# Relative-position attention on one core: heads regrouped by every fourth, the first batch's near terms stored in four parts, and two schedules moved

## The chip, the core and the metric

The kernel runs on one NeuronCore of a Trainium2 chip. That core has TensorE (PE) for matmuls, VectorE (DVE), ScalarE (ACT) and GpSimd (POOL) for elementwise work, SyncE (SP), which issues most of the transfers, and 16 DMA engines between on-chip memory (SBUF, 128 partitions) and HBM. The metric is the device time of one launch in microseconds (us); less is better.

## The reference, cut to what matters

The network is a chain of six sublayers on a token array of 4 batches x 512 tokens x 128 channels. The change touches only the second sublayer, the disentangled attention of layer 0, with 16 heads of 8 channels:

```python
q, k, v = split_heads(x @ Wq + bq), split_heads(x @ Wk + bk), split_heads(x @ Wv + bv)
scores  = einsum('bhqd,bhkd->bhqk', q, k) / scale
pos_k   = (rel_embeddings @ Wk + bk)                       # 64 rows per head
c2p = take_along_axis(einsum('bhqd,hpd->bhqp', q, pos_k), clip(rel + 32, 0, 63), -1)
p2c = take_along_axis(einsum('bhkd,hpd->bhkp', k, pos_k), clip(-rel + 32, 0, 63), -1).swapaxes(-1, -2)
probs = softmax(scores + (c2p + p2c) / scale, -1)          # 4 x 16 x 512 x 512
out = layernorm((probs @ v merged) @ Wo + bo + x)
```

`rel` depends only on the distance of query and key. Within 64 tokens of the diagonal it takes many values ("near"); farther out it is one constant on each side ("far").

## The kernel before

**Tables.** For each batch, 12 matmuls ("chunks", `row_products`) make the position products of q and k, 5 of 112 rows and 1 of 128 rows for each side. ScalarE copies each into one of four `rows` buffers (`copy_rows`) and SP stores it to HBM (`store_chunk`). SP loads them back turned by block (`load_rows`: `load_q_rows`, `load_k_rows`, ten loads or places a batch), so that partition 8h+n holds head h and block n of 64 queries.

**Near terms.** `near_build` adds pairs of these rows into the tile `near`: 128 partitions of 64 x 192 floats, 48 KB each. VectorE builds batch 0, GpSimd batches 1 to 3. The tile goes to HBM (`dram["near"]`): batch 0 by one DMA of 128 rows of 48 KB from SP (`store_first_near`), the others by GpSimd in four pieces of 16 of the 64 queries each (`LATER_PIECES`), and GpSimd waits for every piece before it goes on.

**Attention.** The work is 16 groups n = 4b + g of four heads of one batch; each group is four quads (q = 4n + t, a tile of 128 queries, four heads). For a quad PE makes four score matmuls (`score`), VectorE adds the near terms from `bias` and takes the row maximum (`add_terms`, L1442), ScalarE takes the exponential, PE transposes, PE multiplies with v, VectorE divides (`close_heads`, L1453). SP feeds this: `load_tiles(n)` brings the stacked q and k of a group (128 rows of 2 KB, two buffers), and `load_bias(n, t)` brings the near terms of quad t of group n as two DMAs, each into 64 partitions, 4 heads x 192 floats per partition. `bias` has one buffer for each t, so a load waits until quad t of the group before has been added (`neg_ready`); it thus runs a group ahead.

**Order of the work.** Each engine has one list in order. SP: chunks and row loads of batch 0, `load_tiles(0)`, the near store, a wait for all of it (the store is issued by L1203, the wait is L1249), the eight bias loads of group 0, four more chunks, then the loop over groups and quads, into which `late_quad` puts the 24 chunks of batches 2 and 3 (one after each of the quads 1 to 24) and `ROW_STEPS` the row loads of batches 1 to 3. GpSimd: it waits until batch 0's near store has landed (its build overwrites `near`) and until the first four row loads of batch 1 are there, builds batch 1, stores it, and so on. SP's wait at L1270 stands before the first bias load of batches 1, 2 and 3 and asks for all pieces of that batch.

All of SP's DMAs go into one queue (q1 in the rows below); GpSimd's have a queue of their own (q0). Most move 112 or 128 rows. Two early ones, the zeros that `store_edges` writes into the margins of the tables, have an outermost extent of 6 on both sides (6 x 4 rows of 384 floats, 36 KB each).

## Time and profile before

| | us |
|---|---|
| median of 3 runs (lowest, highest) | 788.75 (788.44, 790.29) |
| the profiled execution | 788.52 |
| its span from first to last instruction | 786.8 |
| busy: PE, DVE, ACT, POOL | 583.0, 531.2, 437.1, 219.6 |
| feed-forward and tables before the attention's quads | 0 to 162 |
| wait for the first near terms | 162 to 180 |
| 64 quads of attention | 180 to 476 |
| the four sublayers after it | 476 to 787 |

The profile page gives one execution. Busy time of an engine says little by itself; the timeline and the waits say which instruction released which. Times in the rows are us from the start of the span.

### The profile page before, as it was taken

The page shows a single profiled execution, that of the slowest core. Times are in us where ns is not written, and L with a number is a line of the kernel's source. Part 1 is how long each engine was busy: PE and PEld are TensorE (multiplying, and loading weights), DVE is VectorE, ACT ScalarE, POOL GpSimd, SP SyncE. Part 2 cuts the span into 40 slices and gives each one's busy share as a digit, 9 for nine tenths or more (in the row PEclk, how much of TensorE's full clock was granted, in tenths as well). Part 3 has the DMA queues.
Part 4 walks back from the last instruction along what each step waited for, and adds up shares of the span by engine and source line. Part 5 has one row for each costly group of instructions (what it writes and reads, how often), then busy time and mean ns, then how long its engine had stood idle before and what let it go on. Part 6 is the DMA issues. An engine that isn't in the chain of part 4 may idle for free. (4 is left out here: it accounts for less than half of the span.)

```text
span 786.8 us, 16609 instructions
## 1 busy us (share of the span) xinstructions
PE 583.0 (74%) x5220; PEld 417.2 (53%) x5220; DVE 531.2 (68%) x1878; ACT 437.1 (56%) x944; POOL 219.6 (28%) x274
## 2 busy tenths in 40 slices
PE   4499927727999999999999998343993661686660
PEld 3387923324666566667666666233982451364460
DVE  7612235815787678989999995771226888766887
ACT  2034524415888788888888884631551523464522
POOL 1743422000950391095040000056442100212000
PEclk9999977866999999999999998655997655799655
DMA  8669525989989899999954413725552000000001
GB/s 251 179 182 391 185 79 169 289 342 269 283 274 335 220 278 348 324 225 271 338 157 129 124 48 99 165 76 146 180 166 71 0 1 1 0 1 2 0 1 53
DMA packets 133602, 130.79 MB, mean 166 GB/s; under 512 B 29565, under 2 KB 109485, under 8 KB 131853
## 3 DMA queue, kind: packets, MB, share of 16 engines
q1 hardware_dynamic: 126668, 103.61, 46.3%
q0 software_dynamic: 4736, 25.07, 8.7%
q10 hardware_dynamic: 2112, 1.05, 0.5%
q8 instruction: 44, 0.72, 0.4%
q14 instruction: 42, 0.34, 0.1%
HBM read 73.43 MB, written 52.92 MB: 161 GB/s over the span
## 5 line engine op out<-in xcount | busy, mean ns | idle before, releaser
L1442 DVE CUSTOM_DVE_ANT_0 l0am_prob<-l0am_ps_s,l0am_bias 128x512 f32<-128x512 f32 x256 | 161.6, 687 | 56.1 <-PE l0am_ps_s L1519 34.9
L1361 ACT ACTIVATE l0am_prob<-l0am_prob,l0am_neg_top 128x512 f32<-128x512 f32 x256 | 172.1, 730 | 19.1 <-DVE l0am_neg_top L1442 19.0
L1531 PE MATMUL l0am_ps_t<-c_ident,l0am_prob 128*128 128x128 f32 x1024 | 138.2, 279 | 0.0
L1531 PEld LDWEIGHTS l0am_ps_t<-c_ident,l0am_prob 128*128 128x128 f32 x1024 | 113.8, 142 | 16.7 <-issue 16.6
L1355 ACT COPY l0am_probT<-l0am_ps_t 128x512 f32<-128x512 f32 x128 | 69.0, 590 | 45.6 <-PE l0am_ps_t L1531 45.6
L1519 PE MATMUL l0am_ps_s<-l0am_ks,l0am_qs 32*128 32x512 f32 x512 | 74.0, 647 | 21.7 <-DVE l0am_neg_top L1442 19.5
L1429 DVE COPY l0am_probT<-l0am_ps_t 128x512 f32<-128x512 f32 x128 | 82.2, 683 | 2.5 <-PE l0am_ps_t L1531 2.4
L764 DVE COPY l0f_xsT<-l0f_psT 128x128 f32<-128x128 f32 x46 | 13.4, 292 | 97.5 <-PE l0f_psT L872 97.5
L593 ACT ACTIVATE l0f_h<-l0f_psU,l0f_experts 128x128 f32<-128x128 f32 x184 | 52.6, 368 | 47.2 <-PE l0f_psU L882 47.2
L1544 PE MATMUL l0am_ps_c<-l0am_probT,l0am_v 128*9 128x128 f32 x2048 | 67.9, 273 | 0.9 <-issue 0.9
L509 POOL DMA_INDIRECT token_results<-l0f_ys,l0f_token_i x46 | 44.3, 962 | 62.5 <-DVE l0f_ys L774 61.9
L882 PE MATMUL l0f_psU<-l0f_xsT,l0f_mine 128*128 128x128 f32 x368 | 55.3, 297 | 4.2 <-issue 1.8
L1142 POOL TENSOR_TENSOR l0am_near<-l0am_rows_q,l0am_rows_k 128x352 f32<-128x352 f32 (+7 forms) x24 | 31.3, 1336 | 96.2 <-DMA l0am_rows_k<-position_k 86.8
L1544 PEld LDWEIGHTS l0am_ps_c<-l0am_probT,l0am_v 128*9 128x9 f32 x2048 | 49.5, 90 | 11.7 <-issue 11.6
L1151 POOL TENSOR_TENSOR l0am_near<-l0am_rows_q,l0am_rows_k 128x192 f32<-128x192 f32 (+6 forms) x96 | 54.0, 608 | 0.2
L882 PEld LDWEIGHTS l0f_psU<-l0f_xsT,l0f_mine 128*128 128x128 f32 x368 | 48.6, 206 | 8.3 <-issue 4.9
L499 POOL DMA_INDIRECT sorted_tokens<-l0f_xn,l0f_pos_i x32 | 31.4, 980 | 56.7 <-DVE l0f_pos_i L665 47.9
L1519 PEld LDWEIGHTS l0am_ps_s<-l0am_ks,l0am_qs 32*128 32x128 f32 x512 | 20.2, 184 | 47.8 <-issue 25.4
L1552 PEld LDWEIGHTS l0am_ps_g<-c_ident,l0am_headT 128*128 128x128 f32 x64 | 9.0, 140 | 48.2 <-issue 28.8
L1481 PE MATMUL l0am_ps_s<-l0am_xnT,l0w_wext 128*112 128x512 f32 (+1 forms) x48 | 27.2, 726 | 4.5 <-ACT l0am_rows L1337 3.8
L893 PE MATMUL l0f_psR<-l0f_experts,l0f_h 128*128 x192 | 27.1, 286 | 1.7 <-ACT l0f_h L593 1.7
L1337 ACT ACTIVATE l0am_rows<-l0am_ps_s,l0w_row_bias 112x512 f32<-112x512 f32 (+1 forms) x24 | 16.1, 687 | 20.6 <-PE l0am_ps_s L1481 7.2
(312 smaller groups left out, 976.6 us busy)
## 6 DMA issues: line engine op xcount, KB each, us to landing
l0am_bias<-near_terms SPq DMA_DIRECT2D x128, 192.0 KB, 4.8
near_terms<-l0am_near POOLq DMA_DIRECT2D x12, 1536.0 KB, 8.3
l0f_mine<-l0f_experts SPq DMA_DIRECT2D x46, 256.0 KB, 2.8
l0am_rows_k<-position_k SPq DMA_DIRECT2D x16, 448.0 KB, 6.9
near_terms<-l0am_near SPq DMA_DIRECT2D x1, 6144.0 KB, 19.8
position_q<-l0am_rows SPq DMA_DIRECT2D x20, 224.0 KB, 4.8
position_k<-l0am_rows SPq DMA_DIRECT2D x20, 224.0 KB, 4.9
l0am_rows_q<-position_q SPq DMA_DIRECT2D x20, 224.0 KB, 6.0
```

What stands on the lines that cost most here:

```text
L499: pool.indirect_dma_start(xs_dram[:, :], bass.IndirectOffsetOnAxis(ap=pos_i[:, t:t + 1], axis=0), xn[:, t, 0:XS_COLS], None).then_inc(scat ...
L509: pool.indirect_dma_start(ys_dram[:, :], bass.IndirectOffsetOnAxis(ap=token_i[:, s:s + 1], axis=0), ys[:, s % UNROLL, :], None).then_inc(y ...
L593: last = nc.scalar.activation(h[:, j, k, :], psU[:, s % 2, k, :], ACT.Gelu_apprx_tanh, bias=part_of(row, SLAB_B1 + k, 1))
L882: last = pe.matmul(psU[:, s % 2, k, :], mine[:, j, k * P:(k + 1) * P], xsT[:, j, :], start=True, stop=True)
L1151: last = engine.tensor_tensor(view(near, at, (WIN + 1, 64), (1, width)), view(rows_q, ROW_OF[pq] * 64, (1, 64), (0, width)), view(rows_k, ...
L1355: nc.scalar.copy(probT[:, u // GROUP % 2, u % GROUP, :, :], ps_t[:, u % 2, :, :]).then_inc(copied_act, 1)
L1361: nc.scalar.activation(prob[:, k, :], prob[:, k, :], ACT.Exp, bias=neg_top[:, k:k + 1], scale=-1.0)\
L1429: dve.tensor_copy(probT[:, u // GROUP % 2, u % GROUP, :, :], ps_t[:, u % 2, :, :]).then_inc(copied_dve, 1)
L1442: dve.tensor_tensor_reduce(out=prob[:, k, :], in0=ps_s[:, j, :], in1=bias[:, j, at:at + S], scale=-1.0, scalar=HUGE, op0=ALU.add, op1=ALU.min,
L1519: pe.matmul(ps_s[:, j, :], qs[r, n % 2, t * P:t * P + P], ks[r, n % 2, :], start=True, stop=True, tile_position=(32 * j, 0)).then_inc(scor ...
L1531: last = pe.transpose(ps_t[:, u % 2, i, :], prob[:, u % SLOTS_, i * P:(i + 1) * P], ident[:, :])
L1544: last = pe.matmul(ps_c[32 * j:32 * j + DH + 1, 0:P], v[:, T4 * b + i, GROUP * g + j, :], probT[:, q % 2, j, i, :], start=(i == 0), stop=( ...
```

## The change

Four things change. (1) A group now holds the heads g, g+4, g+8, g+12 instead of 4g to 4g+3; so `load_tiles`, `load_bias`, the v columns and the place of the result take other strides, and the source of `load_tiles` is now four blocks of 32 rows. (2) Batch 0's near terms go out group by group: `store_first_near(g)` issues four DMAs, one a head, of 8 partitions (rows of 48 KB) each. Group 0's bias loads wait only for its own four; the stores of groups 1, 2 and 3 are issued later in SP's list, and GpSimd waits for all 16 DMAs before it builds batch 1. The first two of batch 1's row loads move ahead of that wait, and the next two to right behind group 0's bias loads. (3) GpSimd's four pieces become two. (4) Batch 3's chunks go to quads 15 to 26 instead of 13 to 24 (quads 13 and 14 get none), and its row loads to 24 to 33 instead of 21 to 30.

```diff
-LATER_PIECES = tuple((q0, q0 + 16) for q0 in range(0, 64, 16))
+LATER_PIECES = ((0, 32), (32, 64))
-    for later, quads in ((1, [-1, -1, 0, 0, 1, 1, 2, 2, 3, 3]), (2, range(9, 19)), (3, range(21, 31))):
+    for later, first, quads in ((1, 2, [-4, -4, 0, 1, 1, 2, 2, 3]), (2, 0, range(9, 19)), (3, 0, range(24, 34))):
         for place, quad in enumerate(quads):
-            steps.setdefault(divmod(quad + T4, T4), []).append((later, place))
+            steps.setdefault(divmod(quad + T4, T4), []).append((later, first + place))
...
+        LAST = 3 * BATCH_CHUNKS
-        first_near_out = sem("first_near_out")
+        first_near_out = [sem(f"first_near_out{g}") for g in range(GROUPS)]
+        FIRST_STORES = GROUP
         def late_quad(cn):
-            return cn - EARLY + 1
+            return cn - EARLY + 1 if cn < LAST else cn - LAST + 15
...
-                def store_first_near():
+                def store_first_near(g):
                     part = 64 * WIN
-                    own = [(part, P), (1, part)]
-                    sp.dma_start(bass.AP(dram["near"].tensor, 0, own), bass.AP(near[:, :].tensor, 0, own)).then_inc(first_near_out, 16)
+                    own = [(part, NB), (1, part)]
+                    for j in range(GROUP):
+                        at = (GROUPS * j + g) * NB * part
+                        sp.dma_start(bass.AP(dram["near"].tensor, at, own), bass.AP(near[:, :].tensor, at, own)).then_inc(first_near_out[g], 16)
...
                     for side, dst in enumerate((qs, ks)):
-                        src = bass.AP(dram["stack"][side].tensor, MARGIN + n * GROUP * 32 * FAR_PITCH, [(FAR_PITCH, P), (1, S)])
+                        b, g = divmod(n, GROUPS)
+                        src = bass.AP(dram["stack"][side].tensor, MARGIN + (b * HEADS + g) * 32 * FAR_PITCH,
+                                      [(GROUPS * 32 * FAR_PITCH, GROUP), (FAR_PITCH, 32), (1, S)])
...
-                        src = bass.AP(dram["near"].tensor, n * GROUP * (NB * 64 * WIN) + (2 * t + s) * (64 * WIN),
-                                      [(WIN, 64), (NB * 64 * WIN, GROUP), (1, WIN)])
+                        src = bass.AP(dram["near"].tensor, (b * HEADS + g) * (NB * 64 * WIN) + (2 * t + s) * (64 * WIN),
+                                      [(WIN, 64), (GROUPS * NB * 64 * WIN, GROUP), (1, WIN)])
...
                 sp.wait_ge(near_dve, 1)
-                store_first_near()
+                store_first_near(0)
+                load_rows(1, 0)
+                load_rows(1, 1)
                 sp.wait_ge(filled, 1)
-                sp.wait_ge(first_near_out, 16)
+                sp.wait_ge(first_near_out[0], 16 * FIRST_STORES)
                 for t in range(T4):
                     load_bias(0, t)
+                store_first_near(1)
...
                             sp.wait_ge(neg_ready, 16 * (n - 1) + 4 * (t + 1))
-                            if g == 0 and t == 0:
+                            if b == 0 and t == 0:
+                                sp.wait_ge(first_near_out[g], 16 * FIRST_STORES)
+                            elif g == 0 and t == 0:
                                 sp.wait_ge(near_out, 16 * len(LATER_PIECES) * b)
                             load_bias(n, t)
-                        for cn in range(EARLY, B * BATCH_CHUNKS):
-                            if n and late_quad(cn) == 4 * (n - 1) + t:
-                                store_chunk(cn)
+                        if (n, t) in ((0, 1), (1, 0)):
+                            store_first_near(2 + n)
+                        if n and T4 * (n - 1) + t in late:
+                            store_chunk(late[T4 * (n - 1) + t])
...
                     if b == 1:
-                        pool.wait_ge(first_near_out, 16)
+                        for g in range(GROUPS):
+                            pool.wait_ge(first_near_out[g], 16 * FIRST_STORES)
...
-                    dve.tensor_tensor(heads_out[:, t, n, :].rearrange("p (j d) -> p j d", j=GROUP), by_head[:, :, 0:DH],
+                    b, g = divmod(n, GROUPS)
+                    own = heads_out[:, t, GROUPS * b:GROUPS * b + GROUPS, DH * g:DH * g + DH]
+                    dve.tensor_tensor(own, by_head[:, :, 0:DH],
...
-                            last = pe.matmul(ps_c[32 * j:32 * j + DH + 1, 0:P], v[:, T4 * b + i, GROUP * g + j, :],
+                            last = pe.matmul(ps_c[32 * j:32 * j + DH + 1, 0:P], v[:, T4 * b + i, GROUPS * j + g, :],
```

PE and ScalarE take the chunk of quad q from the dictionary `late` instead of computing `EARLY + q - 1`.

## Rows read from the trace of the kernel before

**Rows 1.** Windows of three stages: busy us per engine, TensorE clock, DMA share, GB/s.
```profile
156.00:180.00 24.00, 6.89 (x45) 4.72 (x43) 2.77 (x4) 3.41 (x5) 0.00 (x0) 0.69 0.83 325
180.00:264.00 84.00, 81.26 (x888) 50.05 (x892) 63.12 (x185) 67.42 (x125) 30.67 (x44) 0.95 0.97 279
...
346.00:476.00 130.00, 129.90 (x1760) 89.84 (x1759) 123.97 (x373) 113.68 (x217) 29.36 (x39) 1.00 0.61 175
```
**Rows 2.** Timeline of all engines around the start of the attention (start us, us).
```profile
153.82 0.34 SPq L1220 DMA_DIRECT2D l0am_qs<-stacked_q  x1
...
155.69 0.43 SPq L1203 DMA_DIRECT2D near_terms<-l0am_near  x1
...
162.58 1.14 PE L1519 MATMUL l0am_ps_s<-l0am_ks,l0am_qs 32*128 32x512 f32 x8 [0.83 <-issue]
...
175.59 5.28 SPq L1227 DMA_DIRECT2D l0am_bias<-near_terms  x8
180.16 0.69 DVE L1442 CUSTOM_DVE_ANT_0 l0am_prob<-l0am_ps_s,l0am_bias 128x512 f32<-128x512 f32 x1 [17.67 <-DMA l0am_bias<-near_terms]
```
**Rows 3.** Windows while one kind of transfer runs: near-term store, then bias loads.
```profile
158.00:172.00 14.00, 4.89 (x41) 3.82 (x39) 2.77 (x4) 2.55 (x3) 0.00 (x0) 0.75 1.04 446
178.00:184.00 6.00, 1.26 (x8) 0.51 (x8) 2.53 (x8) 2.56 (x4) 0.00 (x0) 0.50 1.10 224
```
**Rows 4.** DMA issues of the whole span: out<-in, count, KB each, us to landing.
```profile
l0am_bias<-near_terms SPq DMA_DIRECT2D x128, 192.0 KB, 4.8
near_terms<-l0am_near POOLq DMA_DIRECT2D x12, 1536.0 KB, 8.3
...
l0am_rows_k<-position_k SPq DMA_DIRECT2D x16, 448.0 KB, 6.9
near_terms<-l0am_near SPq DMA_DIRECT2D x1, 6144.0 KB, 19.8
...
l0am_qs<-stacked_q SPq DMA_DIRECT2D x16, 256.0 KB, 4.4
...
position_q<-in_block_rows SPq DMA_DIRECT2D x1, 36.0 KB
position_k<-in_block_rows SPq DMA_DIRECT2D x1, 36.0 KB
```
**Rows 5.** DMA queues from 97.5 to 98.9 us: packets, MB, share of 16 engines.
```profile
q1 hardware_dynamic: 60, 0.07, 15.2%
```
**Rows 6.** Timeline, VectorE: first reduction of quads 4, 5 and 16.
```profile
200.88 0.69 DVE L1442 CUSTOM_DVE_ANT_0 l0am_prob<-l0am_ps_s,l0am_bias 128x512 f32<-128x512 f32 x1 [1.06 <-PE l0am_ps_s L1519]
...
206.00 0.69 DVE L1442 CUSTOM_DVE_ANT_0 l0am_prob<-l0am_ps_s,l0am_bias 128x512 f32<-128x512 f32 x1 [1.05 <-PE l0am_ps_s L1519]
...
263.68 0.69 DVE L1442 CUSTOM_DVE_ANT_0 l0am_prob<-l0am_ps_s,l0am_bias 128x512 f32<-128x512 f32 x1 [2.35 <-issue]
```
**Rows 7.** Timeline of GpSimd: build and stores of batch 1's near terms.
```profile
197.90 10.45 POOL L1142 TENSOR_TENSOR l0am_near<-l0am_rows_q,l0am_rows_k 128x352 f32<-128x352 f32 x8 [71.75 <-DMA l0am_rows_k<-position_k]
...
226.71 0.61 POOL L1290 DMA_DIRECT2D near_terms<-l0am_near  x1 [0.31 <-POOL l0am_near L1151]
...
251.97 0.53 POOL L1290 DMA_DIRECT2D near_terms<-l0am_near  x1 [7.95 <-DMA near_terms<-l0am_near]
```
**Rows 8.** Timeline of SyncE: the first bias load of batch 1.
```profile
259.40 1.25 SPq L1227 DMA_DIRECT2D l0am_bias<-near_terms  x2
```
**Rows 9.** Waits of SyncE's own queue: us in total, times, longest us.
```profile
SPq L1249 <- DMA near_terms<-l0am_near: 19.4, 1, 19.4
...
SPq L1270 <- DMA near_terms<-l0am_near: 10.6, 3, 8.3
```
**Rows 10.** Timeline, VectorE: closing step of quads 25, 30, then 46 and 47.
```profile
325.46 0.19 DVE L1453 TENSOR_TENSOR l0a_heads<-l0am_ps_g,l0am_rate 128x32 f32<-128x32 f32 x1
...
348.79 0.19 DVE L1453 TENSOR_TENSOR l0a_heads<-l0am_ps_g,l0am_rate 128x32 f32<-128x32 f32 x1
...
416.10 0.19 DVE L1453 TENSOR_TENSOR l0a_heads<-l0am_ps_g,l0am_rate 128x32 f32<-128x32 f32 x1
...
420.32 0.19 DVE L1453 TENSOR_TENSOR l0a_heads<-l0am_ps_g,l0am_rate 128x32 f32<-128x32 f32 x1
```

More of the change, by code:

```diff
@@ L1125, in late_quad @@
         def late_quad(cn):
-            return cn - EARLY + 1
+            return cn - EARLY + 1 if cn < LAST else cn - LAST + 15
+        late = {late_quad(cn): cn for cn in range(EARLY, B * BATCH_CHUNKS)}
         def view(what, offset, *dims):
@@ L1382, in _ @@
                         exp(4 * q + 3)
-                    cn = EARLY + q - 1
-                    if EARLY <= cn < B * BATCH_CHUNKS:
-                        copy_rows(cn, ps_g[:, :])
+                    if q in late:
+                        copy_rows(late[q], ps_g[:, :])
             @block.vector
@@ L1452, in close_heads @@
                     dve.wait_ge(rates_ready, q + 1)
-                    dve.tensor_tensor(heads_out[:, t, n, :].rearrange("p (j d) -> p j d", j=GROUP), by_head[:, :, 0:DH],
+                    b, g = divmod(n, GROUPS)
+                    own = heads_out[:, t, GROUPS * b:GROUPS * b + GROUPS, DH * g:DH * g + DH]
+                    dve.tensor_tensor(own, by_head[:, :, 0:DH],
                                       rate[:, :].unsqueeze(2).broadcast_to((P, GROUP, DH)), ALU.mult).then_inc(heads_ready, 1)
@@ L1556, in _ @@
                         score(q)
-                    cn = EARLY + q - 2
                     if 3 <= q:
-                        if EARLY <= cn < B * BATCH_CHUNKS:
-                            pe.wait_ge(rows_ready, cn + 1)
+                        if q - 1 in late:
+                            pe.wait_ge(rows_ready, late[q - 1] + 1)
                         turn_heads(q - 3)
@@ L1569, in _ @@
                         turn(4 * (q - 1) + 3)
-                    cn = EARLY + q - 1
-                    if EARLY <= cn < B * BATCH_CHUNKS:
-                        if cn == EARLY + 1:
-                            pe.wait_ge(rows_ready, cn)
+                    if q in late:
+                        if late[q] == EARLY + 1:
+                            pe.wait_ge(rows_ready, late[q])
                         if 3 <= q:
                             pe.wait_ge(heads_ready, q - 2)
-                        row_products(cn, ps_g[:, :])
+                        row_products(late[q], ps_g[:, :])
         clear_semaphores(nc, own_sems + aside.own_sems)
```

## The prediction

> **What bounds the kernel now.** I read the windows first. The attention is 64 quads from 180 to 476 us, with PE at 97 to 100% in each window [rows 1], in lockstep with VectorE and ScalarE. A quad takes 4.22 us without table work (416.10 to 420.32 [rows 10]) and 5.12 us with a chunk in it (200.88 to 206.00 [rows 6]). The change removes no chunk, so this pace stays.
>
> What it can move are the waits around it. The timeline shows the first: PE has the first scores at 162.58, but VectorE's first reduction starts at 180.16, after 17.67 us of waiting for a bias load; the load was issued at 175.59, 19.9 us after the near store was issued at 155.69 [rows 2], and SP's queue was waiting for that store for 19.4 us of it [rows 9]. A second is small: SP waits 8.3 us for the near terms of batch 1 [rows 9], issues their load at 259.40 [rows 8], and quad 16 starts at 263.68 [rows 6]. At the usual pace from quad 5 it would be 206.00 + 11 x 5.12 = 262.4, so 1.3 us are lost. A third: quads 26 to 30 took 348.79 - 325.46 = 23.3 us for 5 x 4.22 = 21.1 [rows 10], so 2.2 us are lost.
>
> Behind quad 16 stands a chain: GpSimd starts batch 1's build at 197.90, stores it from 226.71 on (28.8 us of build), and the four stores are through at 259.4, 32.7 us later [rows 7, 8]. From there to quad 16 are 4.3 us. That chain had 4 us to spare at most. GpSimd may start only when all of batch 0 is stored, which is long done before. After the change it isn't.
>
> **The price that decides: a group's store.** It is 4 DMAs of 8 partitions x 48 KB, 1.57 MB. I call its time g. The whole store (6144 KB, 6.29 MB [rows 4]) ran at 446 GB/s [rows 3], 14.1 us for its bytes; the other 5.8 us of its 19.9 were what was queued ahead of it, and its landing. Nothing in the trace stores so few partitions, so I bound it.
>
> - Best: it goes over all 16 engines like the whole one: 1.57 MB at 446 GB/s, g = 3.5 us.
> - Engines: two early DMAs of 24 rows with outermost extent 6 (36 KB each [rows 4]) left 60 packets on q1 [rows 5], 48 rows and 12 more, 6 a DMA. A counting packet from each engine used gives 6 engines, not 16 (with 16 it would be 80 packets). So an outermost extent of 8 gives 8 engines: g = 7.1 us.
> - Worst: the rate also goes by the partitions. While only bias loads run, each into 64 partitions, all engines are as busy as with the store (DMA share 1.10 against 1.04), but move 224 GB/s instead of 446 [rows 3]: half the partitions, half the rate. In proportion, 8 partitions get 27.9 GB/s, so one DMA takes 14.1 us: g = 14.1 if the four run at once, 56.4 if one after another.
>
> The bias row is the nearest one, so I stay with its rule. Between its two readings I take the geometric middle, g = 28.2 us: the four follow one another on the same engines, but a part of the 8 partitions may have a path of its own.
>
> The Trainium skill speaks against this change here. SBUF — State Buffer, section "Door 1: The DMA port swizzle", says that a transfer's rate goes by how many of 16 ports its partitions reach, about 27 GB/s a port, that partitions 0 to 63 reach 8 of them, and by its table an aligned block of 8 reaches 2. The trace agrees for 64 partitions (224 GB/s); for 8 no row here shows it. By it one DMA would take about 7.2 us and, as an estimate, the four in a row 29 us.
>
> **The change part by part.**
>
> *Tile loads.* Their source's outermost extent becomes 4, so by the same reading they use 4 engines: 2 x 256 KB at a quarter of 446 GB/s are 4.7 us instead of 1.2, +3.5. `load_tiles(0)` lies right ahead of the near store in the queue [rows 2], so that much is added there.
>
> *Start.* Group 0 stored: 155.7 + 5.8 + 3.5 + g = 165.0 + g. Then 4.6 us for its bias load (175.59 to 180.16 [rows 2]): with g = 28.2 the first quad is at 197.8, 17.6 us later than now.
>
> *Up to GpSimd's start.* Behind that moment SP's queue holds, in order: group 0's bias, 1.57 MB at 224 GB/s, 7.2 us; store 1, g; four chunks, 0.95 MB at 279 GB/s [rows 1], 3.5; two row loads, 0.67 MB, 2.3; store 2, g; tiles of group 1, 4.7; the first bias of group 1, 1.8; store 3, g. The sum is 19.5 + 3g. The engines that serve the stores serve everything else too, so I let them add. GpSimd's start: 184.5 + 4g = 297.3. It had 197.90.
>
> On the way PE stops twice: group 1's tiles and first bias land near 269.5, but quad 4 wants them at 197.8 + 20.7; the next bias is queued behind store 3, so quad 5 starts at about 300. Both lie in the shade of the next term.
>
> *To quad 16.* Build 28.8 us; stores in two pieces instead of four, 32.7 less two fixed shares of at most 2.7 us (a piece takes 8.3 to land [rows 4], its bytes 5.6 at 279 GB/s), I take 28 us (from 14.1 at 446 GB/s to 32.7 if nothing is won); then 4.3 us. Quad 16 = 245.6 + 4g = 358.4, where it was 263.7: **+94.7 us**. The quads alone would be there at 300 + 11 x 5.12 - 1.8 (two chunks fewer before it) = 354.5, so GpSimd's chain sets it, by 4 us.
>
> *Batch 3's tables.* 12 chunks stay 12 chunks. The two free quads lie in that shade. Row loads three quads later: SP is less crowded at the third wait, worth at most its 2.2 us; I take **-2**. Batch 2 afterwards: GpSimd free at 354, 28.8 + 28 us, 411; quad 32 comes at 358.4 + 11 x 5.12 + 5 x 4.22 = 436, so no new wait. Batch 3: its last rows (quads 32, 33) land by 442, done by 475; quad 48 at 503.
>
> *Regrouping itself.* As many matmuls, adds and bytes; only strides change. 64 closing writes of 0.19 us [rows 10] with another stride: 0, and under 1 us if each took 10% more.
>
> Sum against the profiled execution's 788.5: + 94.7 - 2 = 881. The median of the runs is 0.2 us above it: I write 881.
>
> The formula carries the case: each us of g costs 4. It breaks even at g = 5.0 us (6.8 if the tile loads keep 16 engines).
>
> **Rivals.**
> 1. *All 16 engines, no loss by partitions* (the other side). g = 3.5, tile loads unchanged (-7): quad 16 at 252.6, 11.1 us earlier: 775. For it: the whole store's rows ran at full rate one partition at a time. Against: the 60 packets and the 224 GB/s. It decides from g under 5 us.
> 2. *8 engines only.* g = 7.1: quad 16 at 274, +10: 797. The first quad is then 3.5 us earlier and the gain is lost at GpSimd's late start. Against it: 224 GB/s with all engines busy.
> 3. *Four transfers at once.* g = 14.1: quad 16 at 302, +38 - 2: 825. Against it: one queue, same engines.
> 4. *In full proportion.* g = 56.4: quad 16 at 471: 994.
> 5. *It comes out even*, g near 5: 789.
>
> **How the numbers follow.** Chances: forecast 0.42 (g from 24 to 33: 864 to 900), rival 1 0.21, rival 2 0.12, rival 3 0.14, rival 4 0.04, even 0.07. A measurement of this kernel tells about 0.3% from no change, 2.4 us. Slower 0.42 + 0.12 + 0.14 + 0.04 = 0.72; same 0.07; faster 0.21. The range leaves out rival 4 and most of rival 1: 780 to 900.
>
> **What would show it.** Right: q1's mean rate near 50 to 60 GB/s while SP waits at its first near wait; first reduction near 198; PE waiting twice, for tiles near 218 and for a bias near 275; GpSimd's batch 1 starting near 297; nothing new after quad 16. Wrong: a first reduction near 170 says g is 3.5; near 177, 8 engines at full rate. If stores 1 to 3 overlap with the other traffic instead of adding to it, the slope is under 4 and the loss smaller. A TensorE clock at 0.50 after the long stops, as it is at the start [rows 3], would slow the next quads by a few us more.

## The result and the profile after

| | before | after |
|---|---|---|
| median (lowest to highest), us | 788.99 (788.44 to 790.29) | 913.32 (912.05 to 914.14) |
| profiled execution, us | 788.52 | 912.85 |
| its span, us | 786.8 | 911.1 |
| first reduction of quad 0 | 180.16 [rows 2] | 197.31 |
| of quad 4 | 200.88 [rows 6] | 272.36 |
| of quad 5 | 206.00 [rows 6] | 298.60 |
| of quad 16 | 263.68 [rows 6] | 366.79 |
| GpSimd starts batch 1 | 197.90 [rows 7] | 295.67 |
| quad 16 to quad 63 | 208.8 us | 229.0 us |

Ratio 1.1604, 95% interval [1.1562, 1.1645]: 124.3 us slower by the medians. The forecast was 881, +92.5. The last row of the table is the difference of two first reductions in the timeline (263.68 and 472.52 before, 366.79 and 595.80 after); it was expected to shrink by 2 us and grew by 20.2.

The timeline of SyncE after the change, cut: from the tiles of group 0 to the first bias loads of group 1, and those of group 4, for quad 16 (start us, us of issuing):

```profile
156.04 0.62 SPq L1228 DMA_DIRECT2D l0am_qs<-stacked_q  x1
...
158.47 9.48 SPq L1209 DMA_DIRECT2D near_terms<-l0am_near  x4
168.00 4.90 SPq L1183 DMA_DIRECT2D l0am_rows_q<-position_q  x1
...
192.76 5.62 SPq L1236 DMA_DIRECT2D l0am_bias<-near_terms  x8
198.43 9.88 SPq L1209 DMA_DIRECT2D near_terms<-l0am_near  x4
...
233.18 14.13 SPq L1209 DMA_DIRECT2D near_terms<-l0am_near  x4
247.35 3.52 SPq L1228 DMA_DIRECT2D l0am_qs<-stacked_q  x1
250.91 4.43 SPq L1228 DMA_DIRECT2D l0am_ks<-stacked_k  x1
255.45 7.99 SPq L1236 DMA_DIRECT2D l0am_bias<-near_terms  x2
263.48 7.60 SPq L1209 DMA_DIRECT2D near_terms<-l0am_near  x4
...
280.37 10.05 SPq L1236 DMA_DIRECT2D l0am_bias<-near_terms  x2
...
353.66 1.22 SPq L1228 DMA_DIRECT2D l0am_ks<-stacked_k  x1
354.97 1.71 SPq L1236 DMA_DIRECT2D l0am_bias<-near_terms  x2
```

Between a group's store and the landing the queue is not idle: issuing itself is slow. Four stores take 7.6 to 14.1 us to issue, where the whole store took 0.43 [rows 2], and a row load behind them 4.90. Everything in SyncE's list moves back by that, tiles and bias loads too. What moves meanwhile, in windows (columns as in rows 1):

```profile
170.00:190.00 20.00, 0.00 (x0) 0.00 (x0) 0.00 (x0) 0.00 (x0) 0.00 (x0) 0.50 0.48 68
206.00:230.00 24.00, 3.23 (x49) 1.95 (x48) 2.54 (x9) 0.96 (x2) 0.00 (x0) 0.67 0.56 65
270.00:295.00 25.00, 11.93 (x116) 7.39 (x116) 4.29 (x12) 5.55 (x10) 0.00 (x0) 0.70 0.47 84
```

Half of the DMA engines' time is taken and 65 to 84 GB/s come of it, against 446 GB/s with the whole store [rows 3]; PE does nothing from 170 to 190. The timelines of VectorE, ScalarE and GpSimd show who waited how long, in the brackets:

```profile
197.31 0.69 DVE L1457 CUSTOM_DVE_ANT_0 l0am_prob<-l0am_ps_s,l0am_bias 128x512 f32<-128x512 f32 x1 [32.98 <-DMA l0am_bias<-near_terms]
272.36 0.69 DVE L1457 CUSTOM_DVE_ANT_0 l0am_prob<-l0am_ps_s,l0am_bias 128x512 f32<-128x512 f32 x1 [28.93 <-PE l0am_ps_s L1536]
298.60 0.69 DVE L1457 CUSTOM_DVE_ANT_0 l0am_prob<-l0am_ps_s,l0am_bias 128x512 f32<-128x512 f32 x1 [20.61 <-issue]
366.79 0.69 DVE L1457 CUSTOM_DVE_ANT_0 l0am_prob<-l0am_ps_s,l0am_bias 128x512 f32<-128x512 f32 x1 [6.53 <-PE l0am_ps_s L1536]
...
496.74 0.69 DVE L1457 CUSTOM_DVE_ANT_0 l0am_prob<-l0am_ps_s,l0am_bias 128x512 f32<-128x512 f32 x1 [9.35 <-PE l0am_ps_s L1536]
...
295.67 10.42 POOL L1146 TENSOR_TENSOR l0am_near<-l0am_rows_q,l0am_rows_k 128x352 f32<-128x352 f32 x8 [167.85 <-DMA near_terms<-l0am_near]
324.44 0.61 POOL L1305 DMA_DIRECT2D near_terms<-l0am_near  x1 [0.31 <-POOL l0am_near L1155]
338.04 0.57 POOL L1305 DMA_DIRECT2D near_terms<-l0am_near  x1 [12.99 <-DMA near_terms<-l0am_near]
...
233.33 0.69 ACT L1353 ACTIVATE l0am_rows<-l0am_ps_g,l0w_row_bias 112x512 f32<-112x512 f32 x1 [26.37 <-DMA position_q<-l0am_rows]
```

Up to quad 5 the times are near the forecast's. One stop is new: at 233.33 a table chunk had waited 26.37 us for its `rows` buffer, whose store stood behind the group stores, and PE with it (the window 206 to 230 above). It lies in the shade of quad 4's wait for tiles. At quad 16 the picture differs from the forecast, which had GpSimd's chain end last: SyncE issues quad 16's bias load at 354.97, right behind the tiles, without a wait for GpSimd's stores, and what ends last is PE's wait for tiles (364.68 below). The reduction at 496.74 is quad 40, in the middle of batch 2, where nothing was to happen. Its cause stands one step back, in PE's timeline and in the waits of 196 to 500 us (total, times, longest):

```profile
364.68 2.09 PE L1536 MATMUL l0am_ps_s<-l0am_ks,l0am_qs 32*128 32x512 f32 x8 [4.45 <-DMA l0am_ks<-stacked_k]
411.48 1.36 PE L1536 MATMUL l0am_ps_s<-l0am_ks,l0am_qs 32*128 32x512 f32 x8 [4.27 <-DMA l0am_ks<-stacked_k]
494.64 2.09 PE L1536 MATMUL l0am_ps_s<-l0am_ks,l0am_qs 32*128 32x512 f32 x8 [8.16 <-DMA l0am_ks<-stacked_k]
```

```profile
PE l0am_ps_s L1536 <- DMA l0am_ks<-stacked_k: 50.2, 7, 26.9
```

PE waits seven times for the tiles of a group (`load_tiles`), for over 3 us at quads 4 (the 26.9), 8, 16, 24 and 40, each the first of a group. And the DMA issues show what is odd about these loads (KB each, us to landing):

```profile
l0am_bias<-near_terms SPq DMA_DIRECT2D x128, 192.0 KB, 5.0
near_terms<-l0am_near SPq DMA_DIRECT2D x16, 384.0 KB
l0am_qs<-stacked_q SPq DMA_DIRECT2D x16, 256.0 KB
l0am_ks<-stacked_k SPq DMA_DIRECT2D x16, 256.0 KB
```

Before, the tiles' line had a landing time, 4.4 us [rows 4]. Now it has none, just like the group stores and, before, the two early transfers with an outermost extent of 6 [rows 4], whose packets had told of 6 engines each [rows 5]. The missing time hints at a DMA on fewer than 16 engines, and both the stores (extent 8) and the tiles (extent 4) show it. By itself it is no proof: the loads of parameters at the program's start have none either. The packets of SyncE's queue over the whole span, before and after, say more:

```profile
q1 hardware_dynamic: 126668, 103.61, 46.3%
q1 hardware_dynamic: 126396, 103.61, 44.1%
```

By the prediction's reading (one counting packet from each engine used, [rows 5]) 32 tile loads on 4 engines in place of 16 leave 384 fewer, and 16 stores on 8 engines in place of one on 16 leave 112 more: 272 fewer, which is the difference of these rows to the packet. Each part comes out alone too: 126284 in kernels 3 and 9 below (the tiles only), 126780 in kernels 4, 5 and 6 (the stores only), 126668 still in kernel 1.

The Trainium skill, DMA: Bandwidth & Descriptors, section "Why a DMA increments its semaphore by 16 and not by 1", gives the rule: a DMA uses the largest number of engines, up to 16, that divides the slowest dimension on both sides. The packet counts of this case agree with it, for extents of 4, 6 and 8.

### The profile page after: what moved, and what is told of

Read it like the earlier page. It is cut to its first block and busy times, and to the rows that moved or that the text cites. A ratio compares the mean times of both kernels' runs of the same rounds, so it can differ in the third digit from the quotient of the medians.

```text
span 911.1 us, 16623 instructions
## 1 busy us (share of the span) xinstructions
PE 600.8 (66%) x5220; PEld 426.7 (47%) x5220; DVE 532.4 (58%) x1878; ACT 437.4 (48%) x944; POOL 216.5 (24%) x268
## 5 line engine op out<-in xcount | busy, mean ns | idle before, releaser
L1548 PE MATMUL l0am_ps_t<-c_ident,l0am_prob 128*128 128x128 f32 x1024 | 142.8, 284 | 25.6 <-ACT l0am_probT L1371 25.4
L1548 PEld LDWEIGHTS l0am_ps_t<-c_ident,l0am_prob 128*128 128x128 f32 x1024 | 118.3, 146 | 42.8 <-issue 41.8
L1536 PE MATMUL l0am_ps_s<-l0am_ks,l0am_qs 32*128 32x512 f32 x512 | 78.9, 688 | 85.0 <-DMA l0am_ks<-stacked_k 50.2
L1561 PE MATMUL l0am_ps_c<-l0am_probT,l0am_v 128*9 128x128 f32 x2048 | 70.6, 280 | 0.9 <-issue 0.9
L1498 PE MATMUL l0am_ps_g<-l0am_xnT,l0w_wext 128*112 128x512 f32 (+1 forms) x48 | 26.7, 640 | 19.3 <-DVE l0a_heads L1470 19.3
L1353 ACT ACTIVATE l0am_rows<-l0am_ps_g,l0w_row_bias 112x512 f32<-112x512 f32 (+1 forms) x24 | 16.5, 689 | 29.4 <-DMA position_q<-l0am_rows 26.4
L1498 PE MATMUL l0am_ps_s<-l0am_xnT,l0w_wext 128*112 128x512 f32 (+1 forms) x48 | 26.9, 719 | 4.7 <-ACT l0am_rows L1353 3.9
```

The lines of the kernel that those rows point to most:

```text
L1498: pe.matmul(bank[0:n, :], wext[:, side, k * CHUNK:k * CHUNK + n], xnT[:, T4 * b:T4 * b + T4, :].rearrange("p t q -> p (t q)"), start=True, ...
L1536: pe.matmul(ps_s[:, j, :], qs[r, n % 2, t * P:t * P + P], ks[r, n % 2, :], start=True, stop=True, tile_position=(32 * j, 0)).then_inc(scor ...
L1548: last = pe.transpose(ps_t[:, u % 2, i, :], prob[:, u % SLOTS_, i * P:(i + 1) * P], ident[:, :])
L1561: last = pe.matmul(ps_c[32 * j:32 * j + DH + 1, 0:P], v[:, T4 * b + i, GROUPS * j + g, :], probT[:, q % 2, j, i, :], start=(i == 0), stop= ...
```

## The experiments

The open points: how much of the loss are the slow group stores, how much the tile loads on few engines (theory A in the expectations, theory C in that of kernel 13), how much the two pieces (theory B), the wider strides of the bias loads (rival C), the moved tables; and why a group's store is slow, engines or partitions. Each kernel is compared with the kernel before on the same chip. Two of the chips run the kernel before in 810 us (with quad 0 some 10 us later) and two in 787 to 788, so ratios are compared, not times; the times in the expectations are meant for a kernel before of 789. A difference of ratios times 789 gives microseconds to within a few. The diffs show only the lines that matter. In the table, quad 0 is the start of its first reduction, and 0 to 16 and 16 to 63 are the times from one quad's first reduction to the other's.

| kernel | ratio [95%] | quad 0 | 0 to 16 | 16 to 63 |
|---|---|---|---|---|
| after | 1.1604 [1.1562, 1.1645] | 197.31 | 169.5 | 229.0 |
| 1 before, tile source as 4 x 32 rows | 1.0001 [0.9973, 1.0029] | | | 209.9 |
| 2 before, two pieces | 1.0017 [0.9989, 1.0044] | | | 211.2 |
| 3 before, regrouped | 1.0458 [1.0400, 1.0517] | 193.9 | 91.0 | 232.2 |
| 4 after, neighbouring heads | 1.0781 [1.0721, 1.0841] | 200.37 | 139.4 | 208.9 |
| 5 before, store by eights | 822.06 us to 787.71 | 211.34 | | |
| 6 before, store by spread eights | 834.10 us to 787.71 | 222.05 | | |
| 7 after, whole store | 1.0412 [1.0368, 1.0456] | 182.4 | 91.0 | 228.3 |
| 8 after, four pieces | 1.1542 [1.1494, 1.1591] | 196.8 | 171.8 | 226.9 |
| 9 before, heads padded apart | 1.0496 [1.0442, 1.0550] | | 92.4 | 231.7 |
| 10 regrouped, tiles head by head | 1.0146 [1.0094, 1.0197] | | | 216.4 |
| 11 after, neighbours, one store of 32 | 1.0065 [1.0031, 1.0099] | 172.23 | 93.3 | 208.3 |
| 12 before, 32 partitions, then 96 | 1.0173 [1.0131, 1.0216] | 173.73 | 105.7 | 210.6 |
| 13 after, tiles head by head | 1.1313 [1.1273, 1.1353] | 210.0 | 163.8 | 220.0 |
| 14 before, tables moved | 1.0026 [1.0005, 1.0047] | 189.9 | 82.8 | 209.9 |
| 15 before, the 96 from GpSimd | 1.0140 [1.0106, 1.0175] | 181.2 | 102.5 | 209.1 |
| 16 the same, issued earlier | 1.0098 [1.0066, 1.0130] | 199.7 | 81.5 | 206.6 |

Kernels 5 and 6 ran once each, beside a median of 7 of the kernel before. Kernels 1 to 4, 13 to 16 ran on the chips of 810 us.

### One part of the change at a time

**Kernel 1.** An attempt at the tile loads alone:

```diff
-[(FAR_PITCH, P), (1, S)]
+[(32 * FAR_PITCH, GROUP), (FAR_PITCH, 32), (1, S)]
```

> The kernel before, with one edit: the source of the tile loads is written as 4 blocks of 32 rows instead of 128 rows. Same bytes, same addresses, same heads. Theory A (the 20 us lost after quad 16 come from tile loads that use few DMA engines and are late when GpSimd's stores run): PE gets new waits for the tiles at quads that begin a group, 5 to 20 us in all, 794 to 809. Theory B (they come from GpSimd's larger pieces, rows of 24 KB that hold up SP's queue): no new waits of note, 787 to 791.

No difference, but it tells nothing of the theory: the DMA issues still show a landing time for these loads, 4.9 and 5.6 us, and the queue has the 126668 packets of the kernel before, so they still ran on all 16 engines. The heads lie right behind one another in HBM, 4 x 32 rows are the same addresses as 128, and the two dimensions were evidently joined on the way. Kernel 9 repeats the test with heads that can't be joined.

**Kernel 2.** GpSimd's four pieces become two (rows of 24 KB in place of 12).

```diff
-LATER_PIECES = tuple((q0, q0 + 16) for q0 in range(0, 64, 16))
+LATER_PIECES = ((0, 32), (32, 64))
```

> The kernel before with GpSimd's stores in two pieces instead of four, nothing else. Theory A (tile loads on few engines are the cause): the chain of batch 1 ends 2 to 5 us earlier, quad 16 loses nothing, 786 to 789. Theory B (24 KB rows hold up SP's queue): bias and tile loads land late in the stores of batches 1 to 3, 795 to 810.

No difference. Theory B falls.

**Kernel 3.** Only the strides of the regrouping: `load_tiles`, `load_bias`, the v columns, the place of the result.

```diff
-[(FAR_PITCH, P), (1, S)]
+[(GROUPS * 32 * FAR_PITCH, GROUP), (FAR_PITCH, 32), (1, S)]
...
-[(WIN, 64), (NB * 64 * WIN, GROUP), (1, WIN)]
+[(WIN, 64), (GROUPS * NB * 64 * WIN, GROUP), (1, WIN)]
```

> The kernel before with the heads of a group taken every fourth (tile loads, bias loads, v columns and result with the strides of the change), nothing else. Theory A: as the kernel with only the tile source refactored, within 2 us of it, since the regrouping costs nothing but through the tile loads' few engines. Rival C (the wider strides of the bias loads cost by themselves): 5 us or more above that kernel.

4.6% slower, and quads 16 to 63 take 232.2 us. The part costed at nothing costs 0.0458 x 789 = 36 us without any group store. Theory A and rival C aren't told apart by it, since kernel 1, the yardstick of the expectation, kept its 16 engines; kernel 9 does that.

**Kernel 4.** The other half: the four-part store and all the rest of the change, but on heads 4g to 4g+3 (the diff, against the changed kernel, is cut: tile loads, bias loads, v columns and result have the strides of the kernel before again).

```diff
-at = (GROUPS * j + g) * NB * part
+at = (GROUP * g + j) * NB * part
```

> The changed kernel with groups of four neighbouring heads again, so that tile loads are 128 rows; the group stores stay four DMAs of 8 partitions. Theory A: group 0's store still takes about 28 us, so the first quad is at 193 to 195; GpSimd starts near 289; the waits at the starts of later groups go, and quads 16 to 63 take 207 to 211 us as before; 880 to 890. Theory B: those waits stay, about 905. If the store's price came from the spread of the four heads over the partitions, the first quad would be at 175 to 185.

Quads 16 to 63 are back at 208.9 us, so the late loss comes with the regrouping. In all it costs 0.0781 x 789 = 62 us, less than the 91 to 101 expected (880 to 890). The store costs less than in the changed kernel though the DMAs have the same size and count: quads 0 to 16 take 139.4 us and not 169.5. Some 8 of these 30 us are the tile loads (91.0 in kernel 3 against 83.2 in kernel 1); for the rest, what differs is which partitions the four DMAs of a group read. Windows of this kernel, the second with nothing but its stores and two row loads under way:

```profile
170.00:180.00 10.00, 5.19 (x41) 3.96 (x39) 2.77 (x4) 2.55 (x3) 0.00 (x0) 0.89 0.64 94
180.00:190.00 10.00, 0.00 (x0) 0.00 (x0) 0.00 (x0) 0.00 (x0) 0.00 (x0) 0.50 0.55 122
```

122 GB/s against 68 for every fourth head (170 to 190 us above).

### Why eight partitions are slow

**Kernels 5 and 6.** The kernel before, its near store as 16 DMAs of 8 partitions, next to each other (5; the diff) or 16 apart (6, with `(16 * part, NB)` and `at = h * part`).

```diff
-own = [(part, P), (1, part)]
+own = [(part, NB), (1, part)]
+for h in range(HEADS):
+    at = h * NB * part
```

> The kernel before, with its one near store of 128 partitions split into 16 DMAs of 8 neighbouring partitions each, all waited for. Theory: 8 neighbouring partitions are limited to about 55 GB/s however many engines carry them, so the store takes 16 x 7.1 = 113 us instead of 14 and the first quad comes near 180 + 99 = 279. Rival (8 engines at full rate is all that is lost): 28 us, first quad near 194. Rival (in proportion to the partitions, 28 GB/s): 226 us, first quad near 392.

> As the one before, 16 DMAs of 8 partitions, but the 8 partitions of a DMA stand 16 apart (h, h+16, ..., h+112). Same engines per DMA, same bytes, same row length. If what limits is which partitions share a path into SBUF (the SBUF page's port table gives four paths to such a set), the rate doubles: 58 us for the store, first quad near 224. If it is the number of partitions alone: the same as with neighbours. If it is the engines alone: 28 us in both, first quad near 194.

Windows of kernel 5 (the stores are issued from 157.16 on):

```profile
160.00:170.00 10.00, 5.19 (x41) 3.96 (x39) 2.77 (x4) 2.55 (x3) 0.00 (x0) 0.90 0.39 53
170.00:180.00 10.00, 0.00 (x0) 0.00 (x0) 0.00 (x0) 0.00 (x0) 0.00 (x0) 0.50 0.43 128
180.00:190.00 10.00, 0.00 (x0) 0.00 (x0) 0.00 (x0) 0.00 (x0) 0.00 (x0) 0.50 0.50 192
190.00:200.00 10.00, 0.00 (x0) 0.00 (x0) 0.00 (x0) 0.00 (x0) 0.00 (x0) 0.50 0.48 188
```

and of kernel 6:

```profile
160.00:170.00 10.00, 4.28 (x35) 3.21 (x33) 2.77 (x4) 2.55 (x3) 0.00 (x0) 0.83 0.47 103
170.00:180.00 10.00, 0.00 (x0) 0.00 (x0) 0.00 (x0) 0.00 (x0) 0.00 (x0) 0.50 0.53 118
180.00:190.00 10.00, 0.00 (x0) 0.00 (x0) 0.00 (x0) 0.00 (x0) 0.00 (x0) 0.50 0.51 118
190.00:200.00 10.00, 0.00 (x0) 0.00 (x0) 0.00 (x0) 0.00 (x0) 0.00 (x0) 0.50 0.48 104
```

The share of the engines is about the same half in all (0.39 to 0.53; 8 of 16), the rate is not: it goes by the partitions. Spread eights hold 103 to 118 GB/s steadily; bias loads follow the first issue by 217.69 - 156.97 = 60.7 us, about as expected. Neighbouring eights begin at 53 GB/s, half of that, as expected too, but climb to 192. The 113 us expected for the whole store were wrong: the bias loads follow 206.94 - 157.16 = 49.8 us after the first issue. One such DMA is slow, but the next ones read other partitions. The likely reading is that with the engines out of step several run side by side, up to what 8 engines can do (half of 446 is 223). That the engines drift apart is read from the climb, not shown by itself.

The Trainium skill's page SBUF — State Buffer, section "Door 1: The DMA port swizzle", gives a figure for each: 8 neighbours reach 2 ports, some 54 GB/s, and 8 partitions 16 apart reach 4, some 108. The first windows of both kernels agree (53 and 103). By its formula the heads g and g+4 share their 2 ports and g+8 and g+12 share 2 others, so a group of the changed kernel has 4 ports and a group of neighbours 8; the 68 and 122 GB/s agree in order.

### The changed kernel with one part undone

**Kernel 7.** The whole near store again, everything else as changed.

```diff
-own = [(part, NB), (1, part)]
-for j in range(GROUP):
-    at = (GROUPS * j + g) * NB * part
+own = [(part, P), (1, part)]
```

> The changed kernel with batch 0's near terms stored by one DMA of 128 partitions again; regrouping, two pieces, and the moved tables and row loads stay. The theory says that nearly all of the loss is the group stores; what stays is the tile loads' few engines and whatever the two pieces cost: first quad at 183 to 186, 795 to 815. If the loss after quad 16 is an aftermath of the group stores (queues still full), it goes with them: 788 to 793.

1.0412, 819 us and so 4 us above the expected range. The store by groups carries 0.1604 - 0.0412 = 0.119, 94 us, and what is left, 32 us, is no more than kernel 3 had.

**Kernel 8.** Four pieces again.

```diff
-LATER_PIECES = ((0, 32), (32, 64))
+LATER_PIECES = tuple((q0, q0 + 16) for q0 in range(0, 64, 16))
```

> The changed kernel with GpSimd's stores in four pieces of 12 KB rows again. Theory A (few engines for tile loads): nothing gained, 912 to 920, the waits for tiles stay. Theory B (24 KB rows): most of the 20 us after quad 16 come back, 893 to 900.

0.6 points less, with intervals that overlap; 226.9 us from quad 16 on, where theory B wanted most of the 20 us back. The pieces explain at most 2 of them.

**Kernel 9.** The kernel before with 64 more floats between two heads of the stacked q and k in HBM, and the tile source as in kernel 1. Groups, bias loads, stores and schedules stay.

```diff
+HEAD_PITCH = 32 * FAR_PITCH + 64
...
-MARGIN + n * GROUP * 32 * FAR_PITCH, [(FAR_PITCH, P), (1, S)]
+MARGIN + n * GROUP * HEAD_PITCH, [(HEAD_PITCH, GROUP), (FAR_PITCH, 32), (1, S)]
```

> The kernel before, neighbouring heads, one near store; the heads of the stacked tiles in HBM stand 64 floats further apart, so that a tile load's source is truly 4 blocks of 32 rows. Theory A (tile loads with an outermost extent of 4 run on 4 DMA engines and come late): as the kernel that is only regrouped, 3 to 5% above before, with PE waiting for the tiles at quads 8, 24, 28, 32, 40. Rival C (the regrouping costs by the wider strides of the bias loads or of the result): no difference from before, within 0.5%.

1.0496 and 231.7 us from quad 16 on, as regrouping alone. Its DMA issues and waits:

```profile
l0am_ks<-stacked_k SPq DMA_DIRECT2D x16, 256.0 KB
```

```profile
PE l0am_ps_s L1520 <- DMA l0am_ks<-stacked_k: 21.8, 5, 9.3
```

The landing time is gone, the queue has 384 packets fewer than before (126284), and PE waits for tiles 21.8 us in all (1.4 us before). The outermost extent of 4 in 32 loads is enough for the whole loss; which heads form a group is not needed for it, nor are the strides of the bias loads (rival C), which are here as before.

**Kernels 10 and 13.** The regrouped kernel (3) and the changed kernel with the tiles brought by four DMAs of 32 rows a side.

```diff
-src = bass.AP(..., [(GROUPS * 32 * FAR_PITCH, GROUP), (FAR_PITCH, 32), (1, S)])
-sp.dma_start(dst[:, n % 2, :], src).then_inc(tiles_in[n % 2], 16)
+for j in range(GROUP):
+    src = bass.AP(..., [(FAR_PITCH, 32), (1, S)])
+    sp.dma_start(dst[32 * j:32 * j + 32, n % 2, :], src).then_inc(tiles_in[n % 2], 16)
```

> Every-fourth groups on the kernel before, but a tile load is 4 DMAs of 32 rows, one a head, 8 instead of 2 issues a group. Theory A: the 32 rows go over 16 engines, the waits for tiles are gone, within 1% of before (six more issues of 0.6 us a group on SP). Rival C: still 3 to 5% above before.

> The changed kernel with each group's q and k brought head by head, four transfers of 32 rows a side in place of one of 4 x 32 rows; all else as changed. Theory C (the source's outermost extent of 4 leaves a load to few engines, so the tiles of a group come late): the same edit took the regrouping alone from 1.046 to 1.015 of before, so here TensorE's waits on the k tiles (84 us in all) shrink to what the late near terms leave, and quads 16 to 63, 229.0 us, come down to 212 to 217: 890 to 900 us. The rival (once the near stores are slow the queue is congested anyway, and tiles come late whatever their shape) says within 5 us of the changed kernel's 913.

Kernel 10: 1.0458 becomes 1.0146, somewhat above the 1% expected. Kernel 13: 1.1604 becomes 1.1313, 23 us less by the ratios and 16 by the medians (918.88 to 810.29 is 108.6 slower, the changed kernel 124.3); that is 893 to 898 where before is 789, in the expected 890 to 900. From quad 16 on it takes 220.0 us, 9 less, and more than the 212 to 217 expected. The waits of PE for tiles (of 160 to 560 and 160 to 500 us):

```profile
PE l0am_ps_s L1525 <- DMA l0am_ks<-stacked_k: 3.6, 1, 3.6
```

```profile
PE l0am_ps_s L1537 <- DMA l0am_ks<-stacked_k: 27.0, 2, 24.8
```

In kernel 13 the one of 24.8 us, at quad 4, stays: the tiles stand behind the group stores there whatever their shape. In both a rest remains, 0.0146 x 789 = 12 us in kernel 10, and 11 of the 20 us from quad 16 on in kernel 13. It was not taken apart: 128 transfers in place of 32 have to be issued (in kernel 10's timeline the four of a side take 1.7 to 5.3 us of SyncE's time, where one took 0.3 to 2.2 before), and the bias loads' sources are farther apart.

**Kernel 14.** Batch 3's chunks at quads 15 to 26 and its row loads at 24 to 33, nothing else.

```diff
-            return cn - EARLY + 1
+            return cn - EARLY + 1 if cn < LAST else cn - LAST + 15
...
-(3, range(21, 31))
+(3, range(24, 34))
```

> The kernel before with one part of the change alone: batch 3's chunks at quads 15 to 26 and its row loads at quads 24 to 33. My forecast costed the move at -2 us (a clean quad 13 and 14 ahead of the batch's first load, no new wait). If it is nothing, the ratio is within 0.3% of 1; if batch 3's near terms came late for it, over 1.005 and a wait ahead of quad 48.

1.0026, 2 us slower if anything and not 2 us faster.

### Is there a good way to store by groups?

**Kernel 11.** Kernel 4 with each group stored by one DMA of its 32 neighbouring partitions (the diff is against kernel 4).

```diff
-own = [(part, NB), (1, part)]
-for j in range(GROUP):
-    at = (GROUP * g + j) * NB * part
+own = [(part, GROUP * NB), (1, part)]
+at = g * GROUP * NB * part
```

> The changed kernel with neighbouring heads and each group's store as one DMA of 32 partitions. By the paths into SBUF (32 neighbours reach 8 of 16 by the port table): 218 GB/s, 7.2 us, first quad 7 us before that of the kernel before; GpSimd's start 10 to 15 us later after the first quad than now; in all -4 to +8 us, 0.995 to 1.01. In proportion to the partitions (111 GB/s, 14.1 us): GpSimd starts 35 us later, +20 to +30 us.

From 1.0781 to 1.0065: the same bytes, partitions, order and waits, in 4 DMAs and not in 16. Its timeline:

```profile
155.57 0.43 SPq L1208 DMA_DIRECT2D near_terms<-l0am_near  x1
166.25 6.46 SPq L1232 DMA_DIRECT2D l0am_bias<-near_terms  x8
172.23 0.69 DVE L1453 CUSTOM_DVE_ANT_0 l0am_prob<-l0am_ps_s,l0am_bias 128x512 f32<-128x512 f32 x1 [9.66 <-DMA l0am_bias<-near_terms]
...
205.75 10.44 POOL L1146 TENSOR_TENSOR l0am_near<-l0am_rows_q,l0am_rows_k 128x352 f32<-128x352 f32 x8 [79.12 <-DMA near_terms<-l0am_near]
```

Quad 0 starts 8 us earlier than before, and GpSimd 8 us later (197.90 [rows 7]); quad 16 starts at 265.5, 2 us later. Rival 2 of the prediction had the gain at the start lost at GpSimd's late start. It is lost sooner, at the tiles of group 1, which stand behind the stores:

```profile
199.28 2.09 PE L1530 MATMUL l0am_ps_s<-l0am_ks,l0am_qs 32*128 32x512 f32 x8 [6.29 <-DMA l0am_ks<-stacked_k]
```

Quad 4 starts at 201.39, against 200.88 before. For GpSimd's stores SyncE then waits 1.6 us.

**Kernel 12.** The kernel before with group 0's 32 partitions first and the other 96 behind group 0's bias loads, both from SyncE.

```diff
-store_first_near()
+store_first_near(0, GROUP * NB, first_near_out)
...
     load_bias(0, t)
+store_first_near(GROUP * NB, P - GROUP * NB, rest_near_out)
```

> The kernel before with batch 0's near store in two DMAs: the 32 partitions of group 0 first, the other 96 right behind group 0's bias loads. First store 7.2 us instead of 14.1, the rest 14.5; first quad 6 to 7 us earlier, GpSimd's start about as now (197 to 200), so quad 16 gains only what GpSimd's chain allows: -1 to -4 us, ratio 0.995 to 0.999. If the second store delays the row loads of batch 1, GpSimd starts later and it is even or up to 1% slower.

Quad 0 starts at 173.7, but the ratio is 1.0173, worse than either expectation. The row load behind the big store takes 12.95 us to issue, and a table chunk waits 17.31 us for its buffer:

```profile
185.15 12.95 SPq L1186 DMA_DIRECT2D l0am_rows_k<-position_k  x1
200.70 0.69 ACT L1341 ACTIVATE l0am_rows<-l0am_ps_g,l0w_row_bias 112x512 f32<-112x512 f32 x1 [17.31 <-DMA position_q<-l0am_rows]
```

**Kernels 15 and 16.** Group 0's 32 partitions go out from SyncE, the 96 others through GpSimd's own queue, once quad 0's bias terms have landed (15; the diff) or right after group 0's store (16, where the first wait stays).

```diff
-pool.wait_ge(first_near_out, 16)
+pool.wait_ge(bias_in[0], 32)
+part, first = 64 * WIN, GROUP * NB
+own = [(part, P - first), (1, part)]
+pool.dma_start(bass.AP(dram["near"].tensor, first * part, own),
+               bass.AP(near[:, :].tensor, first * part, own)).then_inc(rest_near_out, 16)
+pool.wait_ge(rest_near_out, 16)
```

> The kernel before with batch 0's near terms stored in two: group 0's 32 neighbouring partitions by SyncE as one transfer, and the other 96 partitions by GpSimd's own queue, once the first quad's bias terms have landed. The last run of this idea lost 1.7% because the big store stood ahead of row loads, chunks and tiles in SyncE's queue. If it is the order of that queue which costs, quad 0 starts near 173.7 as there, quads 0 to 16 take 84 to 88 us in place of 105.7, and the ratio is 0.991 to 0.998. If it is the traffic itself (4.7 MB beside the loads of the first quads), quads 0 to 16 stay above 92 us and the ratio is above 1.002.

> The same, but GpSimd issues its 96 partitions as soon as group 0's store has landed, some 7 us earlier, beside the bias loads of the first quad. If the queues share the engines evenly, the first quad's bias terms come up to 3 us later than in the other (quad 0 at 174 to 177) and the others' earlier; the time is within 0.3% of the other's. If a transfer of 96 partitions holds the engines, quad 0 starts near 182 and nothing is gained over before.

1.0140 and 1.0098. The other queue doesn't help: in kernel 15 a row load takes 11.53 us to issue and the chunk waits 16.39 us, as in kernel 12.

```profile
181.34 0.58 POOL L1312 DMA_DIRECT2D near_terms<-l0am_near  x1 [43.40 <-DMA l0am_bias<-near_terms]
...
193.05 11.53 SPq L1187 DMA_DIRECT2D l0am_rows_k<-position_k  x1
...
207.24 0.69 ACT L1345 ACTIVATE l0am_rows<-l0am_ps_g,l0w_row_bias 112x512 f32<-112x512 f32 x1 [16.39 <-DMA position_q<-l0am_rows]
```

So what costs is the 4.7 MB on the engines, not the order of one queue; the explanation of kernel 12's loss in kernel 15's expectation falls. In kernel 16 the eight bias loads take 20.84 us to issue and quad 0 comes at 199.7, 10 us later than before on such a chip (189.9 in kernel 14): the evenly shared engines of its expectation didn't come about, and the transfer of 96 partitions cost the first quad even more than its other alternative allowed. No version beat the kernel before.

## Why the prediction was wrong

The range (780 to 900) missed by 13 us. By its steps:

- **Time of a group's store**, g = 28.2 us, the geometric middle of 14.1 and 56.4: right in size. The middle of two bounds is no mechanism, so that it came out is partly luck; beside it stood the estimate of 29 from the Trainium skill's port table, and the first window of kernel 5, 53 GB/s, bears that one out. Turned round, quad 0's formula 165.0 + g + 4.6 gives g = 27.7 for 197.31, and GpSimd's 184.5 + 4g gives 27.8 for 295.67. The terms around g were off by 3 us: the store was issued at 158.47, 2.8 us later than assumed, and the bias loads followed at 192.76 all the same, so g may as well be 25. (A slip in the sum: 1.57 MB at 224 GB/s are 7.0 us and not 7.2.)
- **The slope of 4**, stores and other traffic adding up: right up to GpSimd's start (295.67 against 297.3; quad 5 at 298.60 against about 300). Kernel 4 bears it out: from the first store's issue to the bias loads it takes 28.3 us where the changed kernel takes 34.3, and to GpSimd's start (278.65) 111.0 where that takes 137.2, so 6.0 us of g carry 26.2, a slope of 4.4 with the slower tile loads in it. Kernel 7 prices the store by groups at 94 us, the term of the sum at 94.7.
- **What sets quad 16**: "GpSimd's chain sets it, by 4 us" did not hold. That chain was in time (the bias load at 354.97 did not wait for it, and from there quad 16 would have come near the forecast's 358.4), but the quads' own line, forecast to end at 354.5, ended at 366.8; 8 of these 12 us are PE's waits for tiles at quads 8 (3.6 us) and 16 (4.5).
- **Why it is slow**: engines and partitions both. "Against it: one queue, same engines" (rival 3) holds for DMAs that share their paths (kernel 6 stays at 103 to 118 GB/s); in kernel 5 the rate climbs to 192, so others do overlap.
- **The step that failed is the term of the tile loads: "+3.5", counted at two places only (before the first store, and at group 1), while regrouping itself was put at 0 and "nothing new after quad 16" expected.** The engine count was read rightly (4, from the 60 packets), but the price was charged only in the shade of waits that were open anyway, and taken as hidden at the other groups. There are 16 groups. Kernel 3 gives 36 us for the regrouping, kernel 9 39 us for the loads' shape alone, kernel 7 32 us within the changed kernel. Spread over 16 groups that is 2.0 to 2.4 us a group, less than 3.5: the overlap was wrong more than the size. Single waits are longer, 8.2 us at quad 40. That the loads meet eight bias loads and a table's traffic there is a likely reason, not one that a run isolates. In the sum to 913: quad 16 came 8.4 us later than forecast, quads 16 to 63 22.2 us longer (20.2 and the 2 not gained), what follows 1 us; together 31.6 of the 32 missing.
- **Two pieces and moved tables**: costed at up to 4.7 us less in GpSimd's chain and at -2. Kernel 2 shows no difference (1.0017, with an interval across 1), kernel 14 0.26%, 2 us, slower; kernel 8 can't tell four pieces from two. Neither gain came, and what they cost is within 3 us.
- **Rivals**: 1, 2, 3 and 5 needed g from 3.5 to 14, rival 4 56.4; none is near. Kernel 11 has rival 2's early first quad, with the store shape that it takes, and loses it at the tiles of group 1.
- **Signs**: "for tiles near 218" did not come: PE stopped there for a table chunk's buffer (26.4 us, to 233), and for tiles up to 270.

## What to carry to other kernels

Before changing an access pattern, look at the slowest dimension of each side that is left after joining: if it falls from 128 to 4, the load runs on few engines, and its price has to be counted at every use, in the traffic that it meets there. A landing time that vanishes from the DMA issues hints at it in one line, and the queue's packet count confirms it. Bringing the first piece early was worth nothing here (kernels 11, 12, 15, 16), because the rest had to pass through the same engines while others waited for them.

## What the runs showed of the hardware

- The same 6.29 MB, group by group out of the same partitions, cost 56 us of a kernel's time more as 16 DMAs of 8 partitions than as 4 of 32 (kernels 4 and 11, 1.0781 and 1.0065).
- DMAs of 8 neighbouring partitions, one behind the other, go from 53 to 192 GB/s by themselves (kernel 5); of 8 partitions 16 apart they stay at 103 to 118 (kernel 6).
- Two dimensions that are contiguous in HBM are joined before the engines are chosen: 4 x 32 rows kept their landing time, packets and speed (kernel 1), and lost all three with 64 floats between the heads (kernel 9).
- The packet count of a queue tells the engines of its DMAs: it changed by 12 for each load that went from 16 engines to 4, in kernels 3, 7 and 9 (126668 to 126284 for 32 loads).
- Issuing isn't free behind transfers on few engines: 1.9 to 3.5 us a store where the whole store took 0.43, and up to 4.9 for a row load behind.
- A big store in GpSimd's queue holds up SyncE's transfers as much as one in SyncE's own (kernels 12 and 15: 12.95 and 11.53 us to issue the same load).
